# A decoder layer on one core: squares of keys and queries on ScalarE, the keys' scaling on VectorE, the mask laid before the scores

## The reference

```
x = LN(x + Wo . softmax(q k^T / 8) v)            # 16 heads of 64, over x        ("A")
xn, cn = LN(x), LN(context)                      # cross attention               ("B")
q, k, v = xn Wq, cn Wk, cn Wv
k, v = [k, null_k], [v, null_v]                  # one learnt key and value more
q = q / max(|q|, 1e-12) * q_scale                # norm over the 64 of a head
k = k / max(|k|, 1e-12) * k_scale
x = LN(x + LN(softmax(8 q k^T) v . Wo))
x = LN(x + ffn(x)), ffn = causal attention with 16 heads of 8, then 8 experts, top 2   ("C", "M")
... second layer: a small attention over the batch, a gated product with the context, a 4-matrix network
```

## Time and profile before

| | us |
|---|---|
| median of 3 runs | 697.87 (696.43 to 698.28) |
| the profiled execution | 697.76 |
| its span, from first to last instruction | 696.0 |
| TensorE busy | 647.4 (93%) |
| VectorE busy | 463.0 (67%) |
| ScalarE busy | 380.3 (55%) |
| GpSimd busy | 192.9 (28%) |
| mean granted TensorE clock | 0.986 of full |

### The profile page before, as it was taken

How to read it: one execution, slowest core, us unless ns; L and a number is a source line. 1 busy time by engine, 2 the same in 40 slices (tenths; PEclk the granted TensorE clock), 3 DMA queues, 4 the chain that set the end, 5 groups by cost and what they waited for, 6 DMA issues and landing times.

```text
span 696.0 us, 11930 instructions
## 1 busy us (share of the span) xinstructions
PE 647.4 (93%) x4216; PEld 439.0 (63%) x4216; DVE 463.0 (67%) x1298; ACT 380.3 (55%) x1099; POOL 192.9 (28%) x231
## 2 busy tenths in 40 slices
PE   7999999999999999879986879899999999999996
PEld 4676776766767667657663656665767677745543
DVE  2978786875898988988985568684324363584502
ACT  4766566666566766646762466676344345343311
POOL 1221111365565756855134034100000000100101
PEclk9999999999999999999997999999999999999999
DMA  9300000000000000000000000930000000000000
GB/s 283 104 1 1 2 1 1 2 1 1 0 1 2 1 1 1 1 1 2 1 1 1 0 1 2 323 130 1 1 1 0 2 1 1 0 1 0 16 0 15
DMA packets 12729, 15.78 MB, mean 23 GB/s; under 512 B 2168, under 2 KB 9216, under 8 KB 12288
## 3 DMA queue, kind: packets, MB, share of 16 engines
q1 hardware_dynamic: 12384, 14.88, 6.5%
q10 hardware_dynamic: 288, 0.16, 0.1%
HBM read 14.51 MB, written 0.52 MB: 22 GB/s over the span
## 4 chain that ended last, share of the span: by engine, by line
PE 72%; DVE 18%; ACT 6%; issue 2%; POOL 1%; DMA 0%; POOLq 0%; DVEq 0%; SPq 0%; ACTq 0%
PE ring L839 8%; PE ptb L850 8%; PE obank L943 7%; PE ring L916 7%; PE ptb L931 6%; PE ring L868 5%; PE obank L951 4%; PE misc L986 3%; DVE arena L1339 3%; ACT arena L640 3%; PE misc L896 3%; DVE arena L1322 3%; PE misc L897 2%; PE ring L858 2%; PE ring L750 2%; PE ptb L703 2%
## 5 line engine op out<-in xcount | busy, mean ns | idle before, releaser
L640 ACT ACTIVATE arena<-ring,arena 128x256 f32<-128x256 f32 x256 | 129.0, 519 | 5.3 <-DVE arena L1322 5.2
L1339 DVE TENSOR_SCALAR arena<-arena 128x256 f32<-128x256 f32 x256 | 90.7, 399 | 0.0
L1322 DVE TENSOR_REDUCE arena<-ring 128x4 f32<-128x1024 f32 x56 | 68.3, 1220 | 28.6 <-PE ring L916 28.5
L1298 DVE COPY arena<-ptb 128x512 f32<-128x512 f32 x128 | 81.9, 681 | 0.0
L943 PE MATMUL obank<-arena 128*64 128x256 f32 x512 | 72.1, 404 | 3.9 <-ACT arena L616 3.9
L916 PE MATMUL ring<-arena 64*128 64x256 f32 x512 | 73.5, 406 | 0.8 <-ACT arena L640 0.6
L931 PE MATMUL ptb<-ident,arena 128*128 128x128 f32 x512 | 67.8, 276 | 3.2 <-DVE arena L1298 1.8
L578 ACT ACTIVATE arena<-ring,arena 128x512 f32<-128x512 f32 x64 | 42.4, 688 | 49.7 <-PE ring L839 48.5
L931 PEld LDWEIGHTS ptb<-ident,arena 128*128 128x128 f32 x512 | 59.4, 142 | 7.3 <-issue 2.3
L850 PEld LDWEIGHTS ptb<-arena 128*128 128x128 f32 x512 | 59.1, 192 | 3.9 <-issue 3.3
L850 PE MATMUL ptb<-arena 128*128 128x128 f32 x512 | 60.0, 275 | 0.0
(11 more groups left out here) (242 smaller groups left out, 1147.7 us busy)
## 6 DMA issues: line engine op xcount, KB each, us to landing
arena<-in_M_w_dram SPq DMA_DIRECT2D x16, 256.0 KB, 3.8
arena<-in_F_h_dram SPq DMA_DIRECT2D x2, 1024.0 KB, 7.9
arena<-in_B_wkv_dram SPq DMA_DIRECT2D x1, 1024.0 KB, 9.8
arena<-in_F_w_dram SPq DMA_DIRECT2D x3, 256.0 KB, 5.4
rows<-in_rows_dram SPq DMA_DIRECT2D x1, 612.0 KB, 8.5
arena<-in_A_wv_dram SPq DMA_DIRECT2D x1, 512.0 KB, 5.9
x_res<-in_x_dram SPq DMA_DIRECT2D x1, 512.0 KB, 8.5
ctx_tok<-in_ctx_dram SPq DMA_DIRECT2D x1, 512.0 KB, 9.6
```

The costliest lines, as they stand in the source:

```text
L640: ins = nc.scalar.activation(probs[g % 4][:, c, h, :], ring[:, ring_at["S", g, h] % RING, c * S:(c + 1) * S], ACT.Exp, bias=negmax[:, i, q ...
L1298: nc.vector.tensor_copy(probsT[g % 2][:, :, :, c * P:(c + 1) * P].rearrange("p h k q -> p (h k) q"), ptb[:, c, :].rearrange("p (k q) -> p ...
L1322: ins = nc.vector.tensor_reduce(dst[:, i1, q1, :, :].rearrange("p c h -> p h c"), ring[:, r:r + 2, :].rearrange("p h (c k) -> p h c k", c= ...
L1339: ins = nc.vector.tensor_scalar(a, a, rsum[:, i, q, k // 2, k % 2:k % 2 + 1], None, ALU.mult)
```

## The change

Four edits. GpSimd's squares of the key and query pieces go to ScalarE, which makes them with the Square function out of PSUM, ahead of its copy of the same piece; the waits that guarded the buffers go with them. GpSimd's scaling of the keys (khat) goes to VectorE, one step later (s0-4+r), behind a new semaphore `krn_ready`. The mask matrix grows to 384 columns (causal, zeros, causal), and the mask products come before the scores: those of banks 0 and 1 in the step before, ahead of the third round of transposes, those of banks 2 and 3 ahead of the scores, each waiting for its bank to be free. The scores are added to it. GpSimd builds the matrix with two affine_selects.

```diff
-        causal, identb = sb("causal", [P, P], BF16), sb("identb", [P, P], BF16)
+        causal, identb = sb("causal", [P, P + S], BF16), sb("identb", [P, P], BF16)
...
-                    pool_extras[s0 - 5 + r].append(("khat", b, r))
+                    dve_extras[s0 - 4 + r].append(("khat", b, r))
...
 # ScalarE
                         if kind == "K":
                             if b >= 3 and r == 0:
                                 act.wait_ge(misc_done, misc_at["pair", PAIRS * (B + b - 2) - 1] + 1)
+                            if r >= 2 or b >= 1:
+                                act.wait_ge(ksum_part, 4 * b + r - 1)
+                            else:
+                                act.wait_ge(null_ready, 1)
+                            nc.scalar.activation(ksq[:, r % 2, :, :].rearrange("p h a -> p (h a)"), src, ACT.Square).then_inc(ksq_ready, 1)
                             nc.scalar.copy(ktok[b % 3][:, c, hf * 512:(hf + 1) * 512], src).then_inc(ring_free, 1)
                         elif kind == "Q":
                             if b >= 2 and r == 0:
                                 act.wait_ge(ring_done, ring_at["S", PAIRS * (B + b - 1) - 1, 1] + 1)
-                            nc.scalar.copy(qT_all[b % 2][:, 2 * r:2 * r + 2, :], src.rearrange("p (a s) -> p a s", a=2)).then_inc(ring_free, 1)
+                            if b >= 1 and r == 0:
+                                act.wait_ge(misc_done, misc_at["sq", b - 1, 0] + 1)
+                            src = src.rearrange("p (a s) -> p a s", a=2)
+                            nc.scalar.activation(qsq[:, 2 * r:2 * r + 2, :], src, ACT.Square).then_inc(qsq_ready, 1)
+                            nc.scalar.copy(qT_all[b % 2][:, 2 * r:2 * r + 2, :], src).then_inc(ring_free, 1)
...
 # TensorE, narrow attention
+                def mask(g, r):
+                    if g >= 1:
+                        pe.wait_ge(c_ring_free, G * (g - 1) + r + 1)
+                    nc.tensor.matmul(ring[:, r, 0:SW], identb[:, :], causal[:, :], start=True, stop=False, skip_group_check=True)
...
+                        for r in range(0 if s == 0 else 2, G):
+                            mask(s, r)
                         for c, cols_c in enumerate((slice(0, P), slice(P, SW))):
                             for r in range(G):
-                                if s >= 1 and c == 0:
-                                    pe.wait_ge(c_ring_free, G * (s - 1) + r + 1)
                                 lanes = slice(RG * r, RG * (r + 1))
-                                nc.tensor.matmul(... start=c == 0, stop=c == 1, skip_group_check=True)
-                        for r in range(G):
-                            nc.tensor.matmul(ring[:, r, :] ..., identb[:, :], causal[:, :] ..., start=False, stop=True).then_inc(c_ring_done, 1)
+                                ins = nc.tensor.matmul(... start=False, stop=True, skip_group_check=True)
+                                if c:
+                                    ins.then_inc(c_ring_done, 1)
...
+                    if 0 <= s < NGR - 1:
+                        mask(s + 1, 0)
+                        mask(s + 1, 1)
                     if CT <= s < NGR + CT:
                         narrow_tiles(s - CT, 2)
...
 # VectorE
+                        elif kind == "khat":
+                            n = CB * H // 4
+                            dve.wait_ge(krn_ready, b + 1)
+                            k3 = ktok[b % 3][:, :, :].rearrange("p c (h a) -> p (c h) a", a=A)[:, n * r:n * r + n, :]
+                            nc.vector.tensor_tensor(k3, k3, krn[:, n * r:n * r + n].unsqueeze(2).broadcast_to([P, n, A]), ALU.mult)\
+                                .then_inc(khat_ready, 1)
...
 # GpSimd: the squares (L1513 to L1527) and the scalings (L1554 to L1558) go
-                            nc.gpsimd.tensor_tensor(ksq[:, r % 2, :, :], k2, k2, ALU.mult).then_inc(ksq_ready, 1)
...
-                            nc.gpsimd.tensor_tensor(qsq[:, 2 * r:2 * r + 2, :], q2, q2, ALU.mult).then_inc(qsq_ready, 1)
...
-                            ch.step(nc.gpsimd.tensor_tensor(krn[:, :], kss[:, :], half[:, 0:CB * H], ALU.pow))
+                            nc.gpsimd.tensor_tensor(krn[:, :], kss[:, :], half[:, 0:CB * H], ALU.pow).then_inc(krn_ready, 1)
```

More of the change, by code:

```diff
@@ L263, in decoder @@
         pt_done, pt_free, o_done, o_free = sem("pt_done"), sem("pt_free"), sem("o_done"), sem("o_free")
+        krn_ready = sem("krn_ready")
         khat_ready, ksum_ready = sem("khat_ready"), sem("ksum_ready")
@@ L744, in narrow_step @@
                             pe.wait_ge(ring_free, len(ring_at))
+                        for r in range(0 if s == 0 else 2, G):
+                            mask(s, r)
                         for c, cols_c in enumerate((slice(0, P), slice(P, SW))):
                             for r in range(G):
-                                if s >= 1 and c == 0:
-                                    pe.wait_ge(c_ring_free, G * (s - 1) + r + 1)
                                 lanes = slice(RG * r, RG * (r + 1))
-                                nc.tensor.matmul(ring[:, r, cols_c], qTc[lanes, b % 2, c * P:(c + 1) * P], kzn[lanes, b % 2, q, 0:(c + 1) * P],
-                                                 start=c == 0, stop=c == 1, skip_group_check=True)
-                        for r in range(G):
-                            nc.tensor.matmul(ring[:, r, :].rearrange("p (x k) -> p x k", k=P)[:, 0:3:2, :], identb[:, :],
-                                             causal[:, :].unsqueeze(1).broadcast_to([P, 2, P]), start=False, stop=True,
-                                             skip_group_check=True).then_inc(c_ring_done, 1)
+                                ins = nc.tensor.matmul(ring[:, r, cols_c], qTc[lanes, b % 2, c * P:(c + 1) * P], kzn[lanes, b % 2, q, 0:(c + 1) * P],
+                                                       start=False, stop=True, skip_group_check=True)
+                                if c:
+                                    ins.then_inc(c_ring_done, 1)
                     for e in c_first[s]:
@@ L1460, in _ @@
                 ch.step(nc.gpsimd.memset(causal[:, :], 0.0))
-                nc.gpsimd.affine_select(out=causal[:, :], in_=causal[:, :], compare_op=ALU.is_ge, fill=MASKED,
-                                        base=0, pattern=[[-1, P]], channel_multiplier=1)
+                for k in (0, 2):
+                    nc.gpsimd.affine_select(out=causal[:, k * P:(k + 1) * P], in_=causal[:, k * P:(k + 1) * P], compare_op=ALU.is_ge, fill=MASKED,
+                                            base=0, pattern=[[-1, P]], channel_multiplier=1)
                 nc.gpsimd.tensor_copy(identb[:, :], ident[:, :])
```

## The result

The changed kernel takes 738.53 us (median of 4 runs, 738.28 to 739.3) against 697.15 for the kernel before, measured beside it (4 runs, 695.37 to 698.28): ratio 1.0598, 95% interval 1.0572 to 1.0624, +41.4 us. The forecast was 731 (712 to 745): direction and mechanism held, the size is 7.5 us short. The profiled execution took 738.63, its span is 736.9 against 696.0, +40.9; the mean granted clock fell from 0.986 to 0.958. So the profile holds the whole difference.

A forecast was written before the change was run, and what follows sets the result against it. TensorE was taken to bound the first 185 us, TensorE and VectorE together the next 180. Stalls 30.2, clock 10.4, relief -7, other squares +0.5 and mask -1 gave +33.1 on 697.87: 731 us, range 712 to 745 (8 in 10).

The forecast's parts named there:

- The stalls: Wide stages: ScalarE's squares of key pieces 2 and 3 wait for a buffer slot, delaying TensorE eight times: 30.2 us.
- The clock: TensorE behind each of the eight idle times: lower granted clock, 1.3 us a time (bounds nothing and 2.0), 10.4 us.
- The relief: Wide stages: VectorE instructions no longer lengthened beside GpSimd's, less the scalings VectorE gets: -7 us, bounds -14.7 and 0.
- The mask: Narrow attention, sixteen steps: mask products ahead of the scores, -0.3 to +0.15 us each; -1 us taken, bounds -5 and +3.
- The other squares: 8 key and 16 query pieces without such a wait; one or two may show in the second stage: +0.5 us, bounds 0 and 6.
- (a): First wide stage: TensorE's room covers the wait, so only the second stage counts: 690 us, faster; 4%.
- (b): First wide stage: its stalls are filled by later slack and the gain reaches its bound: within 0.3%; 2%.
- (c): Same eight TensorE stalls without clock loss: 10.4 us less, 721; part of the forecast's case, together 88%.
- (d): ScalarE, wide stages: Square lies outside Exp's table, two loads about each of 32 squares: 26 us on top, 757; 3%.
- (e): VectorE's key scalings wait out GpSimd's powers on the port, up to 5 us in each of four batches: 740 to 750; 3%.

The follow-up runs named there:

- four slots: The changed kernel with four slots instead of two in the buffer `ksq` for the squares of keys: 689.18 us, ratio 0.987 to the kernel before.
- the wait alone: The kernel before, with ScalarE made to wait for the sum over squares before copying key pieces 2 and 3, no work moved: 733.23 us, ratio 1.0525.
- products in the idle times: The changed kernel with 3 to 5 useless TensorE matmuls ahead of each of the eight late products, the waits kept: 721.98 us, ratio 1.0364.
- with three: The changed kernel with three slots instead of two in the buffer `ksq` for the squares of keys: 689.96 us, ratio 0.9896.
- batch 0 stalled alone: The changed kernel with four `ksq` slots, but the old early wait for key pieces 2 and 3 of batch 0 only: 698.64 us, ratio 1.0028.

## Why the prediction was right, and where it was short

**The stalls: right.** Predicted 3.0, 3.0, 3.6, 3.6, 8.5 and 8.5 (30.2); read 2.94, 3.08, 4.01, 3.77 and two times 4.69 + 4.09 = 8.78, together 31.4 (sizes from the trace after, cause from four slots and from the wait alone). The square took 0.60, and from its start to the end of L615 (L614 before) it was 1.72 us (124.62 to 126.34) where I had 0.5 + 1.24.

**The clock: the term that was mis-sized.** Predicted 1.3 a time, 10.4, lowered from the 1.6 of the earlier trace rows "because some of the slow time will fall where TensorE waits anyway". Measured: 16.5 (products in the idle times) to 18.6 (what the idle times leave of the 50.0), 2.1 to 2.3 a time. Two steps failed. The price was read from one stretch of 4 us, and the low clock can outlast it: behind 126.40 the first 4 us stood at 0.50 and the next 4 at 0.67, 2.0 + 1.3 us. And it was lowered, but no slack took the slow time up: the stalled steps lost their idle times and the clock's price in full. The bound of 2.0 a time was too low as well; singly the price went from 1.4 to 3.6. By span, stalls 1.2, clock 8.2 and relief -2.3 over what I had said, what follows the last group at +0.5 where I had the mask at -1 and the other squares at +0.5, and the start 0.35 ahead make the 7.8 of 40.9 - 33.1. Open: what decides how long the clock stays low. Idle times of 2.4 us cost 1.7 each with the wait alone, and one of 2.94 cost 3.1 in the changed kernel and nothing in the profiled execution with batch 0 stalled alone.

**The relief: right, a little small.** Predicted -7; read -9.3 in the changed kernel and measured -9.0 with four slots. The mean of L1339 between 185 and 365 us was 434 ns before and is 378 with four slots. The scalings cost what I said: 0.68 each, and in a row the next instruction starts 0.60 behind. What I had too small is the gain: with them went the alternation with the squares on GpSimd, which I had priced as lengthened VectorE instructions and not as a square that TensorE gets late.

**The mask: no weight.** Predicted -1; measured a ratio of 1.0007, whose interval holds no change, and 0.1 us with four slots. The step that failed is that the two products moved forward "wait for two pairs of exponentials, which end before the copies that those transposes wait for": TensorE waited 3.9 us for those exponentials at the mask products, so the wait for the bank took the place of what went from between scores and minimum.

**The other squares at +0.5:** not told apart from zero; four slots has them all and is faster.

**Rivals.** (a) relief wins: 690 against 738.5, out; yet four slots shows that it needed just one more slot, 690.0 with three. (b) it cancels: out. (c) stalls without clock, 721: out for the changed kernel, and what the kernel with filled idle times shows, 722. (d) table loads: the groups show the same eighteen loads as before, all at lines outside the wide stages; Square shares Exp's set here. (e) the scalings wait out the powers: all engines in order of time, the changed kernel, of which GpSimd's power and VectorE's:

```profile
334.98 5.45 POOL L1561 TENSOR_TENSOR arena<-arena,const 128x32 f32<-128x32 f32 x1
...
335.54 0.16 DVE L1364 TENSOR_TENSOR arena<-arena 128x4 f32<-128x4 f32 x1
...
336.23 0.16 DVE L1372 TENSOR_TENSOR arena<-arena 128x4 f32<-128x4 f32 x1
...
342.44 0.68 DVE L1428 TENSOR_TENSOR arena<-arena 128x512 f32<-128x512 f32 x1
```

Inside the power from 334.98 to 340.43 two-input VectorE operations took 0.16, and the scaling (L1428) found the result ready. Against the rule of the Trainium skill ("SBUF — State Buffer", section "SBUF: two separate sides"), that such an operation and a GpSimd instruction exclude each other until the holder ends, the measurement decides for this power (as far as GpSimd's recorded spans go, which are rough); for GpSimd operands of 128x512 the trace of before agreed with it.

## What to carry to other kernels

Moving work to an engine moves its waits: before a wait goes onto an engine that others depend on, list what is queued behind it and compare when its signal comes with when that queue is needed. Here one slot too few turned a gain of 7 to 9 us into a loss of 41. Where TensorE bounds, price an idle time of 3 to 5 us at its length and some 2 us of lower clock on top, and don't discount it.

## What was not expected of the hardware

- Behind idle times of 2.9 to 4.7 us the granted clock stood at 0.50, the level of 1.2 GHz, for the stretches shown, and with the wait alone it fell behind idle times of 2.4 us too. It did not fall each time, and executions of one kernel differ by it: with batch 0 stalled alone, the profiled one lost 7.6 us in its two stalled steps, the timed ones 11.0 by their ratio. Of those twelve, the four with a mean granted clock of 0.985 took 696.4 to 697.0 us, the four with 0.983 698.0 to 698.9, the four with 0.978 700.3 to 702.5. Stretches of 8 us behind the two idle times in that profile, 2.94 and 3.08 us long, the first at the full clock:

```profile
126.17:134.17 8.00, 6.46 (x40) 4.50 (x40) 4.43 (x13) 2.73 (x11) 2.72 (x4) 1.00 0.00 0
...
135.71:143.71 8.00, 8.00 (x44) 5.76 (x46) 2.32 (x7) 5.15 (x17) 0.00 (x0) 0.81 0.01 2
```

- Useless products in an idle time made the kernel 16.5 us faster than leaving TensorE idle.
- A float32 product of 128x512 takes 0.87 us in a row at the full clock.
- 10.9 us more work on VectorE, the second most loaded engine, with 16 fewer GpSimd instructions beside it, made the kernel 5.2 us faster.
